# A transformer block's attention output: softmax sums divided per block through DRAM instead of through a selection matrix

## What is computed

```
ada = silu(c) @ W_ada + b_ada
shift_msa, scale_msa, gate_msa, shift_mlp, scale_mlp, gate_mlp = split(ada, 6)
h = layernorm(x) * (1 + scale_msa) + shift_msa
q, k, v = split(h @ W_qkv + b_qkv)                 # 16 heads of 36
o = softmax(q * 36**-0.5 @ k.T) @ v                # per head, 2048 x 2048 scores
x = x + gate_msa * (o @ W_proj + b_proj)
h = layernorm(x) * (1 + scale_mlp) + shift_mlp
x = x + gate_mlp * (gelu(h @ W_fc1 + b_fc1) @ W_fc2 + b_fc2)
```

## Time and profile before

| | |
|---|---|
| median of 3 runs | 3257.01 us |
| the profiled execution, its own time | 3255.73 us |
| span of its trace | 3254.0 us |
| TensorE busy | 3238.2 us, 100% of the span |
| VectorE, ScalarE, GpSimd busy | 2161.4, 1695.6 and 358.3 us (66, 52 and 11%) |
| granted TensorE clock over the span | 0.999 |
| moved by DMA | 299.5 MB, 92 GB/s |

### The profile page before, as it was taken

How to read it: one execution, slowest core, us unless ns; L and a number is a source line. 1 busy time by engine, 2 the same in 40 slices (tenths; PEclk the granted TensorE clock), 3 DMA queues, 4 the chain that set the end, 5 groups by cost and what they waited for, 6 DMA issues and landing times. The chain is left out here.

```text
span 3254.0 us, 52481 instructions
## 1 busy us (share of the span) xinstructions
PE 3238.2 (100%) x19049; PEld 2117.3 (65%) x19049; DVE 2161.4 (66%) x4134; ACT 1695.6 (52%) x3183; POOL 358.3 (11%) x284
## 2 busy tenths in 40 slices
PE   9999999999999999999999999999999999999999
PEld 7888744444444444444444444449998898989988
DVE  6444488888888888888888888857633433433332
ACT  4323377777777777777777777765611112211110
POOL 0000010111100000010000000026411010000000
PEclk9999999999999999999999999999999999999999
DMA  7554442333323232323232333328722122421211
GB/s 241 179 165 149 153 93 59 75 74 76 66 59 66 59 65 56 68 63 69 59 69 59 65 63 65 63 63 276 238 95 77 53 82 71 142 69 57 80 46 55
DMA packets 187841, 299.53 MB, mean 92 GB/s; under 512 B 66783, under 2 KB 87791, under 8 KB 180670
## 3 DMA queue, kind: packets, MB, share of 16 engines
q1 hardware_dynamic: 187582, 296.17, 34.1%
HBM read 193.99 MB, written 101.43 MB: 91 GB/s over the span
## 5 line engine op out<-in xcount | busy, mean ns | idle before, releaser
L1306 DVE TENSOR_REDUCE q_mx<-b_st 128x1 f32<-128x512 f32 x1512 | 988.6, 681 | 147.8 <-PE b_st L1240 142.8
L1380 ACT ACTIVATE b_pt<-b_st 128x512 f32<-128x512 f32 x2048 | 1055.1, 609 | 8.6 <-PE b_st L1256 8.5
L1268 PE MATMUL b_op<-b_pt,b_vs 128*37 128x512 f32 x4096 | 981.5, 600 | 2.1 <-DVE b_ob L1349 2.1
L1373 ACT ACTIVATE b_early<-b_st 128x512 f32<-128x512 f32 x504 | 302.3, 600 | 451.3 <-PE b_st L1240 451.3
L1268 PEld LDWEIGHTS b_op<-b_pt,b_vs 128*37 128x37 f32 x4096 | 203.5, 113 | 444.3 <-issue 360.2
L2125 PE MATMUL d_pm<-d_vh,d_ah 128*128 128x288 f32 x1152 | 339.3, 295 | 0.8 <-DVE d_al L2163 0.8
L2126 PE MATMUL d_pm<-d_vl,d_ah 128*128 128x288 f32 x1152 | 339.5, 295 | 0.0
L2127 PE MATMUL d_pm<-d_vh,d_al 128*128 128x288 f32 x1152 | 339.5, 295 | 0.0
L1306 DVE TENSOR_REDUCE q_mx<-b_early 128x1 f32<-128x512 f32 x504 | 339.4, 673 | 0.0
L1444 POOL TENSOR_TENSOR w_oc<-b_oa,b_ob 37x512 f32<-37x512 f32 x127 | 161.3, 1270 | 1440.4 <-DVE b_ob L1349 1437.4
L1240 PEld LDWEIGHTS b_st<-q_hh,b_qa 36*128 36x128 f32 x1024 | 128.7, 184 | 223.5 <-DVE q_mx L1306 197.7
(11 more groups left out here) (414 smaller groups left out, 4685.7 us busy)
## 6 DMA issues: line engine op xcount, KB each, us to landing
qkh<-a_th SPq DMA_DIRECT2D x72, 256.0 KB, 2.1
qkl<-a_tl SPq DMA_DIRECT2D x72, 256.0 KB, 2.3
d_yi<-y SPq DMA_DIRECT2D x64, 288.0 KB, 3.0
n_oi<-hw SPq DMA_DIRECT2D x12, 1024.0 KB, 5.8
vd<-a_vx SPq DMA_DIRECT2D x8, 1184.0 KB, 6.6
b_vs<-vd SPq DMA_DIRECT2D x32, 296.0 KB, 3.0
a_x<-in_x SPq DMA_DIRECT2D x8, 1152.0 KB, 6.8
q_qs<-qkh SPq DMA_DIRECT2D x32, 288.0 KB
```

Source lines behind the costliest of these rows:

```text
L1268: ins = e.matmul(op[64 * a:64 * a + VW, :], vs[h % 2][:, j + 8 * a, :], pt[g % NP][:, a * 512:a * 512 + 512], start=j == 0, stop=j == 7)
L1306: e.tensor_reduce(mx[:, k // 2, col:col + 1], src, AX.X, ALU.max).then_inc(s_mx, 1)
L1373: e.activation(early[:, :], bank(slot)[:, :], ACT.Copy).then_inc(s_cp, 1)
L1380: e.activation(pt[g % NP][:, a * 512:a * 512 + 512], bank(k)[:, :], ACT.Exp, scale=SCALE).then_inc(s_p, 1)
```

## The change

The selection matrix, `rr`, the 64-row inverses and all 40 `turn` matmuls go, with their VectorE multiplications. Each block is divided by itself, over four DMAs that SyncE issues in a row and waits for in between, and by a second GpSimd instruction. A tile `gap` takes the place of the tiles that are gone, so that the tiles behind keep their addresses.

```diff
+    def sums_out(self, e, n, sm):
+        hd, cols = self.rows(n)
+        e.wait_ge(self.s_oc, n + 1)
+        e.dma_start(sm[hd:hd + 1, cols], self.oc[n % 2][D:D + 1, :]).then_inc(self.s_sm, 16)
+        e.wait_ge(self.s_sm, 16 * (n + 1))
+        e.dma_start(self.sr[:, :], sm[hd, cols].rearrange("(p f) -> p f", f=16)).then_inc(self.s_sr, 16)
+    def invert(self, e, n):
+        e.wait_ge(self.s_sr, 16 * (n + 1))
+        e.reciprocal(self.rc[:, :], self.sr[:, :]).then_inc(self.s_rc, 1)
+    def quotients_in(self, e, n, rm):
+        hd, cols = self.rows(n)
+        e.wait_ge(self.s_rc, n + 1)
+        e.dma_start(rm[hd, cols].rearrange("(p f) -> p f", f=16), self.rc[:, :]).then_inc(self.s_rm, 16)
+        e.wait_ge(self.s_rm, 16 * (n + 1))
+        e.dma_start(self.rb[:, :], rm[hd, cols].partition_broadcast(D)).then_inc(self.s_rb, 16)
+    def divide(self, e, n):
+        oc = self.oc[n % 2]
+        e.wait_ge(self.s_oc, n + 1)
+        e.wait_ge(self.s_rb, 16 * (n + 1))
+        e.tensor_tensor(oc[0:D, :], oc[0:D, :], self.rb[:, :], ALU.mult).then_inc(self.s_od, 1)
+    def store(self, e, n, ot):
+        e.wait_ge(self.s_od, n + 1)
+        e.dma_start(ot[hd * D:hd * D + D, cols], self.oc[n % 2][0:D, :]).then_inc(self.s_o[n % 2], 16)
...
@@ the steps of attention
-        s.turn = s.b - LAST - 1 if s.b is not None and LAST < s.b <= LAST + KT else None
-        s.turned = None if s.turn is None else use("turn", s.turn)
+        s.summed = (hb - 7) // 4 if hb > 6 and hb % 4 == 3 and hb < NHB - 1 else None
+        s.inverse = (hb - 8) // 4 if hb > 7 and hb % 4 == 0 and hb < NHB else None
+        s.over = (hb - 9) // 4 if hb > 8 and hb % 4 == 1 else None
@@ attention, sync
             if s.late is not None:
                 max_rows(s.late)
+            if s.inverse is not None:
+                W.quotients_in(e, s.inverse, rm)
             if s.hb < NHB:
...
                 if r == 4 and h + 1 < NH:
                     load_v(h + 1)
+            if s.over is not None:
+                W.store(e, s.over, ot)
             if s.block is not None:
-                e.wait_ge(s_oc, s.block + 1)
-                e.dma_start(ot[hd * D:hd * D + D, cols], oc[i][0:D, :]).then_inc(s_o[i], 16)
-                e.dma_start(sm[hd:hd + 1, cols], oc[i][D:D + 1, :]).then_inc(s_o[i], 16)
+                W.sums_out(e, s.block, sm)
@@ attention, tensor
-            if s.turn is not None:
-                turn(s.turn, s.turned)
@@ attention, vector, at the end of a step
-            if s.block == INV:
-                W.invert(e, 0)
+            if s.summed is not None:
+                W.invert(e, s.summed)
@@ attention, gpsimd, at the beginning of a step
+            if s.over is not None:
+                W.divide(e, s.over)
             if s.block is not None:
...
                 e.tensor_tensor(oc[i][:, :], oa[i][:, :], ob[i][:, :], ALU.add).then_inc(s_oc, 1)
@@ projection, sync
         load(1)
-        rest.store(e, ot, sm)
-        for i in range(2):
-            e.wait_ge(W.s_o[i], 32 * 2 * NH)
-        W.load_sums(e, 1, sm)
...
+            elif kind == "project" and (c, n) == (0, 0):
+                W.quotients_in(e, rest.n - 2, rm)
+            elif kind == "project" and (c, n) == (0, 1):
+                W.sums_out(e, rest.n - 1, sm)
+            elif kind == "project" and (c, n) == (0, 3):
+                W.store(e, rest.n - 2, ot)
+            elif kind == "project" and (c, n) == (0, 4):
+                W.quotients_in(e, rest.n - 1, rm)
+            elif kind == "project" and (c, n) == (0, 6):
+                W.store(e, rest.n - 1, ot)
@@ projection, vector, scalar and gpsimd
-                e.tensor_tensor(af[k % 3][:, :], u[:, :], oi[i][:, n, :], ALU.mult).then_inc(s_u, 1)
-                e.activation(ah[i][:, n, :], af[k % 3][:, :], ACT.Copy).then_inc(s_ah, 1)
+                e.activation(ah[i][:, n, :], oi[i][:, n, :], ACT.Copy).then_inc(s_ah, 1)
...
+                if (c, n) == (0, 3):
+                    W.invert(e, rest.n - 1)
...
+                if (c, n) in ((0, 2), (0, 5)):
+                    W.divide(e, rest.n - (2 if n == 2 else 1))
```

More of the change, by code:

```diff
@@ L167, in load_sums @@
[L167 to L179, removed]
@@ L1270, in products @@
             ins.then_inc(s_pv, 1)
-        def turn(kt, slot):
-            e.wait_ge(W.s_sel, 5)
-            e.wait_ge(W.s_rr, 32 * HCH)
-            bank_free(e, slot)
-            e.matmul(bank(slot)[:, :], W.sel[:, kt, :], W.rr[:, 0, :], start=True, stop=True).then_inc(W.s_ta, 1)
         for s in plan:
@@ L1286, in tensor @@
                 products(2 * s.now)
-            if s.now is not None:
                 products(2 * s.now + 1)
-            if s.turn is not None:
-                turn(s.turn, s.turned)
     def vector(e):
@@ L1482, in phase_proj @@
     xn = A.sb("xn", [128, 4, 640])
-    af = [A.sb(f"af{i}", [128, CH]) for i in range(3)]
     st = [A.sb(f"st{i}", [128, 4, 2, 6]) for i in range(2)]
@@ L1498, in phase_proj, with tokens @@
     SPARE = NCH - 1
-    def turn(c):
-        return [("turn", c, kt) for kt in range(KT)]
+    def tokens(c):
+        return [("tokens", c, kt) for kt in range(KT)]
     def norm(c):
@@ L1556, in work @@
             yield p
-    slots = [(kind, c * KT + kt) for kind, c, kt in work() if kind in ("turn", "back")]
+    slots = [(kind, c * KT + kt) for kind, c, kt in work() if kind == "back"]
     place = {k: n for n, k in enumerate(slots)}
@@ L1564, in turned_free @@
         if n >= 0:
-            was, j = slots[n]
-            if was == "turn":
-                e.wait_ge(s_u, j + 1)
-            elif j // KT in (0, SPARE):
+            j = slots[n][1]
+            if j // KT in (0, SPARE):
                 e.wait_ge(s_hl, split(j // KT) + j % KT + 1)
@@ L1594, in load @@
             if c > 1:
-                e.wait_ge(s_u, KT * (c - 1))
+                e.wait_ge(s_al, KT * (c - 1))
+            if c == HCH:
+                for i in range(2):
+                    e.wait_ge(W.s_o[i], 16 * 2 * NH)
             W.load_tokens(e, c, oi[c % 2], ot)
@@ L1666, in tensor @@
             i, k = c % 2, c * KT + n
-            if kind == "turn":
-                if n == 0:
-                    e.wait_ge(W.s_rr, 32 * (HCH if c < HCH else 2 * HCH - (c < NCH - 1)))
-                turned_free(e, kind, k)
-                e.matmul(pt[place[kind, k] % 4][:, :], sel[:, n, :], W.rr[:, c % HCH, :], start=True, stop=True).then_inc(
-                    s_ta, 1)
-            elif kind == "back":
+            if kind == "back":
                 e.wait_ge(s_xn, 4 * (c + 1))
@@ L1726, in low_h @@
                                 ALU.subtract).then_inc(s_hl, 1)
+        W.invert(e, rest.n - 2)
         rest.evict_even(e)
         for kind, c, n in work():
-            i, k = c % 2, c * KT + n
-            if kind == "turn":
-                u = pt[place[kind, k] % 4]
-                e.wait_ge(s_ta, k + 1)
-                if n == 0:
-                    e.wait_ge(s_a[i], 48 * (c // 2 + 1))
-                if k > 2:
-                    e.wait_ge(s_al, k - 2)
-                e.tensor_tensor(af[k % 3][:, :], u[:, :], oi[i][:, n, :], ALU.mult).then_inc(s_u, 1)
-            elif kind == "project":
+            i = c % 2
+            if kind == "project":
                 m, t, cs = 8 * c + n, n // 2, slice(n % 2 * HALF, n % 2 * HALF + HALF)
@@ L1837, in gpsimd @@
             k = c * KT + n
-            if kind == "turn":
+            if kind == "tokens":
                 e.wait_ge(s_ah, k + 1)
```

149 lines of the change are left out of this document (40 added, 109 removed).

## The result

The changed kernel takes **3670.8 us** (median of 6 runs, 3667.4 to 3675.66) against 3257.23 us of the kernel before (6 runs, 3255.65 to 3257.64), a ratio of 1.127 with a 95% interval of 1.1257 to 1.1286. The forecast was 3715 us, 3400 to 3850. The profiled execution took 3667.4 us.

What follows compares the result with a forecast made beforehand. The prediction took TensorE, busy 3238.2 of 3254.0 us, as the bound. From 3255.7 it took 9.6 and 2.1, added 312 for stalls, 152 for the clock and 5.6 for the projection: 3713.6, so 3715 us for the median, range 3400 to 3850.

Steps and rivals of the forecast that it cites:

- Two of the signs given: Signs that would show the forecast right: attention 440 to 470 us longer, projection shorter by a few us.
- The chain in a quiet period: In attention periods without loads, the transfers before VectorE's reciprocal close with 0.2 us to spare and cost nothing.
- Behind the loads: In attention, the reciprocal comes 7.2 us late behind load A, 3.7 behind load B; TensorE loses 312 us in all.
- the slack: In attention, VectorE can be 0.55 us later before its copies of the output blocks without costing TensorE time.
- Why they are late: In attention, the sum row is written behind the loads in SyncE's ring and waits until that queue is empty.
- The clock: In attention, each of 61 TensorE stalls sets the granted clock back and costs 2.5 us more, 152 us in all.
- the waits that went: TensorE's waits in attention for the copy `ob`, 2.1 us in all, go with VectorE's multiplications and long reciprocal.
- the rival of stalls without a clock: In attention, the waits are as forecast but the clock dips lie inside them; 3563 us, chance 0.25.
- The start of the projection: At the projection's first chunk, `rb` lands at 15.4 us and GpSimd's division holds up the split pieces; costs 5.6 us.
- The chain longer than its period: In attention, the transfers take longer than the period everywhere, so quiet periods are late too; 3790 us, chance 0.12.

Runs made afterwards that it cites:

- independent dose in the kernel before: Kernel before, without the change, with VectorE kept busy by filling an unused tile 15 times behind load A and 12 behind load B; 3753.95 us.
- run 60: Not a run's label: of the 66 clock dips in the whole profiled run of the changed kernel (3667.4 us), 60 are 6.8 us long.
- e6: Changed kernel with loads A and B issued by GpSimd, behind its addition, instead of by SyncE; 3614.29 us, ratio 1.1093.
- spread chain: Changed kernel with the sums, quotients, division and store spread over more steps and a third output buffer; 3263.86 us, ratio 1.0014.
- e7: Changed kernel with a block's four small transfers issued and awaited by GpSimd, while the loads stay with SyncE; 3595.71 us, ratio 1.1041.

## Why the prediction was right

The range, which was wide, and the sign held, and the mechanism was the predicted one but for why the sum row is late. Two of the signs given did not come: attention is 403 us longer, not 440 to 470, and the projection is not shorter. By the steps of the prediction:

- **The chain in a quiet period** closes, as forecast. `sr` lands in 1.5 us, not the 1.8 taken from a larger transfer, so there was a little more room.
- **Behind the loads**: forecast 7.2 and 3.7 us late, lost 6.9 and 3.4, in all 312 us. Measured: waits for `sr` of 6.0 us on average behind A and about 4.6 behind B, 323 us without those of the last blocks, where VectorE has nothing else to do. With 61 reciprocals (15 us) and less the slack (61 x 0.55 = 33.5) it is 305. A was taken too long and B too short, and they cancelled: that 312 and 305 are so near is luck.
- **Why they are late** was put down to the order in SyncE's queue. This step did not hold as it stands: from another engine's queue the small transfer waits as long (7.1 and 8.4 us), if in 16 pieces. Had I been right, moving the loads to GpSimd would have given 3270 us; it gave 3614. The Trainium skill (DMA: Bandwidth & Descriptors, Queues, rings and completion order) speaks of order within a ring, which the prediction used. The same section has a DMA engine take turns between its queues, a whole packet at a time, and lets a semaphore's increment land only after every earlier write of that DMA engine, across its queues. That the delay crosses queues agrees with these rows; by which of the two rules is not shown, but packets that begin 6.9 us late aren't the second alone.
- **The clock** was the term that was mis-sized: 2.5 us a stall forecast, 152 in all. What is left of the 403.2 us of attention, with 3.3 us added back for the five `turn`s and the waits that went, is 406.5 - 305 = 102 us, 1.7 a stall; the independent dose in the kernel before gave 1.5. A dip with nearly each stall was right (60 of 61 pauses; of the 66 dips of the whole run 60 are 6.8 us long), as was that part of it lies in the idle time, and so the rival of stalls without a clock, 3563 us, is out. The lateness and the clock overlap: TensorE's own rows book 226 us as waits and 188 us (178.4 + 9.6) as longer matmuls, since it still has work queued when VectorE stops and lacks it afterwards. Both views give the same sum within 8 us.
- **The start of the projection** was forecast 5.6 us dearer and a few us shorter in all. It came out 8.4 us longer: the division of block 126 starts 13.4 us in (2600.59; I said 15.4), and TensorE loses 3.6 us of its 15.0 there, but some 13 us more are lost at later chunks. The missing step was to ask whether transfers would keep up with a projection that needs less of TensorE.
- **The chain longer than its period** (3790 us) is out: the quiet periods have no waits. That it was near can be seen in `e6`, where each period of a head is a little late.

Summed: 305 + 102 - 1.2 - 2.1 - 8.4 + 16.8 = 412, against 411.6 measured. This must agree, since 102 and 16.8 are what was left over; the check on the clock's share is the dose in the kernel before and TensorE's own rows. The forecast's 44 us too many are some 50 too many for the clock and 7 for the lateness, against 11 too few for the projection.

No version here beats the kernel before; the spread chain comes within 0.14% of it.

## What to carry to other kernels

A small transfer that nobody waited for cost nothing here; once someone waited, it cost what the bulk loads issued before it held up, from SyncE's queue and from GpSimd's. So leave a step or more between issue and wait for each link that can stand behind a load, rather than looking for a better place for the loads; then shortening the engine that looked like the bound is worth only what the next bound leaves, and a dose of useless work shows that in one run.

## What the runs showed of the hardware

- A one-row write goes on 0.9 us after the end of its issue in a quiet period, and 7.4 and 5.7 us behind the eight loads A and B, on SyncE's queue; on GpSimd's it is 1.4, 8.4 and 7.1 us (medians of the changed kernel and of `e7`).
- Over TensorE's pauses of 1 to 5.5 us in attention the granted clock mostly falls to 0.50 (1.2 GHz) near their end: in the changed kernel 41 of 61 times before TensorE works again. With VectorE kept busy instead, it fell 1.2 us before the end of most pauses of 4.25 us and 3.4 us before that of most of 5.9 us. A stall cost 1.5 to 1.7 us beyond its lateness, whether a transfer or a busy VectorE caused it.
- GpSimd issues a transfer of the loads in 0.51 us, SyncE in 0.37 (medians of `e6` and of the changed kernel).
